# Window attention in a two-stage transformer kernel: the masks are added by VectorE in PSUM instead of by TensorE, with a new order of the work on the engines

## What is computed

```python
qkv = x @ Wqkv
q, k = l2norm(q) * qs, l2norm(k) * ksc
q = q * cos * scale + rotate_half(q) * sin * scale
k = k * cos * inv + rotate_half(k) * sin * inv
...
mask = (it < jb) | (it > jb + w) | (jb == -1)
sim = jnp.einsum('bhwie,bhwje->bhwij', bq, bk2) * QK_SCALE
sim = jnp.where(mask, -jnp.finfo(sim.dtype).max, sim)
attn = jax.nn.softmax(sim, -1)
out = jnp.einsum('bhwij,bhwje->bhwie', attn, bv2)
```

## Time and profile before

| | us |
|---|---|
| median of 3 runs (range) | 3487.71 (3485.86 to 3488.28) |
| time of the profiled execution | 3485.04 |
| its span, first to last instruction | 3483.2 |
| PE matmul busy, of the span | 3410.3 |
| DVE busy | 2991.3 |
| ACT busy | 3056.1 |
| POOL busy | 2494.3 |

### The profile page before, as it was taken

The page is one execution under the profiler, slowest core; times in us unless marked ns, Lnnn a source line. Parts: engine busy times, 40 slices in busy tenths (PEclk is TensorE's granted clock), DMA queues, the critical chain, the costliest instruction groups (busy, mean ns, idle before and its releaser), DMA issues. The chain is left out here.

```text
span 3483.2 us, 177745 instructions
## 1 busy us (share of the span) xinstructions
PE 3410.3 (98%) x70388; PEld 2881.8 (83%) x70388; DVE 2991.3 (86%) x7016; ACT 3056.1 (88%) x10549; POOL 2494.3 (72%) x2057
## 2 busy tenths in 40 slices
PE   8999999999999999999999999999999999999998
PEld 5666677888888888888888888888888888888877
DVE  8999988888888888888888888888888888888886
ACT  8999978898988888888888888888888889888886
POOL 0121178887878878788787887878888788887874
PEclk9999999999999999999999999999999999999999
DMA  2000011111211111121111121111211111111111
GB/s 105 8 5 20 5 53 53 48 42 43 57 55 50 44 44 46 54 57 48 46 44 50 52 57 47 43 42 54 59 48 46 43 47 54 45 46 47 51 42 44
DMA packets 177474, 160.59 MB, mean 46 GB/s; under 512 B 113933, under 2 KB 124813, under 8 KB 176397
## 3 DMA queue, kind: packets, MB, share of 16 engines
q1 hardware_dynamic: 176653, 149.22, 15.2%
HBM read 25.71 MB, written 4.19 MB: 9 GB/s over the span
## 5 line engine op out<-in xcount | busy, mean ns | idle before, releaser
L1544 POOL TENSOR_TENSOR a_rn<-a_ssqc,a_minus_half 128x16 f32<-128x16 f32 x384 | 1113.4, 2900 | 256.3 <-DVE a_ssqc L1751 252.1
L1428 ACT ACTIVATE late<-bank,a_negmax 128x64 f32<-128x64 f32 x3072 | 963.9, 343 | 31.0 <-DVE a_negmax L1705 29.4
L1562 POOL TENSOR_TENSOR a_r<-a_u,a_rn 128x512 f32<-128x512 f32 x768 | 800.7, 1043 | 55.9 <-DVE a_u L1733 10.5
L1428 ACT ACTIVATION_READ_ACCUMULATOR late<-bank,a_negmax 128x1 f32 x3072 | 728.6, 237 | 0.0
L1717 DVE TENSOR_TENSOR a_u<-bank,a_rot_c 128x512 f32<-128x512 f32 x768 | 524.7, 683 | 175.3 <-ACT a_sq L1404 174.7
L1551 POOL TENSOR_TENSOR a_PN<-late,a_erec 128x256 f32<-128x256 f32 x768 | 487.9, 636 | 255.8 <-DVE a_erec L1758 241.4
L1726 DVE TENSOR_TENSOR a_v<-bank,a_rot_s 128x512 f32<-128x512 f32 x768 | 522.7, 681 | 0.0
L1733 DVE TENSOR_TENSOR a_u<-a_u,a_v 128x1024 f32<-128x1024 f32 x384 | 469.7, 1223 | 25.6
L1404 ACT ACTIVATE a_sq<-bank 128x512 f32<-128x512 f32 x768 | 462.8, 647 | 17.2 <-PE bank L1013 16.7
L1411 ACT ACTIVATE a_QK<-bank 128x512 f32<-128x512 f32 x768 | 465.8, 607 | 4.1 <-PE bank L1054 1.9
L1054 PE MATMUL bank<-ident,a_r 128*128 128x128 f32 x3072 | 463.3, 274 | 5.2 <-ACT late L1396 1.8
(11 more groups left out here) (190 smaller groups left out, 7757.2 us busy)
## 6 DMA issues: line engine op xcount, KB each, us to landing
a_V_sh<-a_V_nat SPq DMA_DIRECT2D x384, 192.0 KB, 2.5
a_V_sh<-a_V_nat SPq DMA_DIRECT2D x192, 64.0 KB, 2.4
late<-in_qkv SPq DMA_DIRECT2D x20, 384.0 KB, 3.7
...
```

Of the source, the lines that this page charges most:

```text
L1428: ins = act.activation(E[:, s.par, k, :], scores[:, hp, col:col + KW], ACT.Exp, bias=negmax[:, s.par, k:k + 1], accum_out=esum[:, s.par, k ...
L1544: pool.tensor_tensor(rn[:, a.par, :], ssqc[:, a.par, :], minus_half[:, :], ALU.pow).then_inc(S["rn"], 1)
L1562: pool.tensor_tensor(heads(r[:, a.par, half]), heads(u[:, a.par, half]), rn[:, a.par, mm * 2 * HG:(mm + 1) * 2 * HG].unsqueeze(2).to_broad ...
```

## The change

PE no longer writes the masks; the products of queries and keys now overwrite (`start=True`). DVE has a new instruction per pair, `mask`: it adds a float32 mask (kept in SBUF, loaded as float32, the bf16 copies are gone) to the two banks of scores in place, in PSUM, and `maxima` then waits for it (`masked`). Since one mask now serves 128 rows, the table `windows` holds for the first half of a sequence the first window's form in the first 32 rows. All `cycle` functions but POOL's and SP's have a new order. `sines` of a tile now come ahead of `cosines`, so that `project` also waits for `u_rot`.

```diff
@@ -1007,6 +1002,7 @@
                         pe.wait_ge(S["w_lo"], G * a.layer + a.g + 1)
                     ge(pe, S[f"sq{mm}"], a.k)
                     ge(pe, S[f"v_rot{mm}"], a.k)
+                    ge(pe, S["u_rot"], 2 * a.k - 1 + mm)
                     x, m = n % 2, slice((2 * a.half + mm) * P, (2 * a.half + mm + 1) * P)
                     pe.matmul(p_qk[mm][:, :], xh[:, x, m], wh[:, a.g, 0:2 * CQ], start=True, stop=False)
                     pe.matmul(p_qk[mm][:, :], xl[:, x, m], wh[:, a.g, 0:2 * CQ], start=False, stop=False)
...
@@ -1110,11 +1106,6 @@
                     if s.k == 0:
                         pe.wait_ge(S["pads"], 2)
                     sides = (slice(0, 64), slice(64, P))
-                    for c in range(4):
-                        for e in range(2):
-                            rows = slice(WIN * c, WIN * c + WIN)
-                            pe.matmul(scores[rows, e, :], ident_b[sides[e], 64 * e:64 * e + WIN],
-                                      masks[sides[e], int(s.half > 0 or c > 0), :], start=True, stop=True, skip_group_check=True)
...
@@ -1123,7 +1114,7 @@
                                 for e in range(2):
                                     ins = pe.matmul(scores[WIN * c:WIN * c + WIN, e, col:col + KW],
                                                     QK[sides[e], s.gpar, hp, WIN + first:WIN + first + WIN],
-                                                    QK[sides[e], s.gpar, 2 + hp, first:first + KW], start=False, stop=True,
+                                                    QK[sides[e], s.gpar, 2 + hp, first:first + KW], start=True, stop=True,
                                                     skip_group_check=True)
                     ins.then_inc(S["logits"], 1)
...
@@ -1149,30 +1140,31 @@
                 late_end(n, p)
                 outputs(pair_at(n, p, LAG_O), n * NP + p, done(n, p - 1, LAG_T1))
                 project(n, p, 0)
+                if p == P_VALUES:
+                    up(n, p, 0, 1, p_ta)
+                if p == P_X:
+                    up(n, p, 2, 1, p_ta)
+                if p == P_VALUES:
+                    up(n, p, 1, 1, p_tb)
+                if p == P_GATES:
+                    up(n, p, 1, 0, p_ta)
                 if p == P_GATE:
                     up(n, p, 0, 0, p_ta)
-                if p == P_X:
-                    up(n, p, 2, 1, p_ta)
-                project(n, p, 1)
+                if p == P_X and n + 1 < NI:
+                    transpose_x(n + 1)
+                values(n, p)
                 if p == P_TURN:
                     turn(n)
-                if p == P_VALUES:
-                    up(n, p, 0, 1, p_ta)
-                if p == P_GATES:
-                    up(n, p, 1, 0, p_ta)
-                values(n, p)
                 late_pieces(n, p)
                 if p == P_BIAS:
                     shifts(n)
-                if p == P_X and n + 1 < NI:
-                    transpose_x(n + 1)
-                if p == P_VALUES:
-                    up(n, p, 1, 1, p_tb)
                 if p == P_GATES:
                     up(n, p, 2, 0, p_tb)
                 if p == P_GELU:
                     down(n)
+                project(n, p, 1)
                 if s:
+                    ge(pe, S["exp0"], s.k)
                     ge(pe, S["exp1"], s.k)
                 logits(s, p_s)
...
@@ -1443,32 +1436,32 @@
                     late_outputs(2 * p - 1)
                 queries_and_keys(pair_at(n, p, LAG_Q1), 1)
                 exps(s, 0, 0, p_s)
-                exps(s, 0, 1, p_s)
                 queries_and_keys(pair_at(n, p, LAG_Q0), 0)
                 exps(s, 1, 0, p_s)
                 outputs(pair_at(n, p, LAG_O))
+                exps(s, 0, 1, p_s)
+                squares(n, p, 0)
+                if p == P_X and n + 1 < NI:
+                    high_x(n + 1)
                 exps(s, 1, 1, p_s)
+                if p == P_GATE:
+                    gate_out(n, 0, p_ta)
+                if p < 2:
+                    split_up(n, p)
                 if p == P_TURN:
                     turned(n)
-                squares(n, p, 0)
                 if p == P_GATES:
                     gate_out(n, 1, p_ta)
                 if p == P_GELU:
                     gelu(n)
-                if p == P_GATE:
-                    gate_out(n, 0, p_ta)
-                squares(n, p, 1)
-                if p == P_GATES:
-                    gate_out(n, 2, p_tb)
-                if p == P_X and n + 1 < NI:
-                    high_x(n + 1)
-                values(n, p)
-                probs(pair_at(n, p, LAG_PT))
-                if p < 2:
-                    split_up(n, p)
                 split = split_at(n, p)
                 if split:
                     split_qkv(*split)
+                if p == P_GATES:
+                    gate_out(n, 2, p_tb)
+                values(n, p)
+                squares(n, p, 1)
+                probs(pair_at(n, p, LAG_PT))
...
@@ -1698,9 +1691,16 @@
                     dve.wait_ge(S["w_hi"], G * layer + g + 1)
                     low_weights(dve, A, raw[:, g % 2, :], g).then_inc(S["w_lo"], 1)
 
+            def mask(s, scores):
+                if s:
+                    dve.wait_ge(S["logits"], s.k + 1)
+                    dve.tensor_tensor(scores, scores, masks[:, int(s.half > 0), :].unsqueeze(1).to_broadcast([P, 2, 4 * KW]),
+                                      ALU.add).then_inc(S["masked"], 1)
+
             def maxima(s, scores):
                 if s:
-                    dve.wait_ge(S["logits"], s.k + 1)
+                    dve.wait_ge(S["masked"], s.k + 1)
+                    ge(dve, S["exp0"], s.k - 1)
                     ge(dve, S["exp1"], s.k - 1)
                     dve.tensor_reduce(negmax[:, s.par, :].rearrange("p (b i) -> p b i", b=2), scores.rearrange("p b (i k) -> p b i k", i=4), AX.X,
                                       ALU.max, negate=True).then_inc(S["max"], 1)
...
@@ -1720,7 +1720,10 @@
             def sines(a, mm):
                 if a:
                     m = 2 * a.half + mm
+                    dve.wait_ge(S[f"sq{mm}"], a.k + 1)
                     ge(dve, S["u"], a.k)
...
@@ -1780,40 +1783,41 @@
 
             def cycle(n, p):
                 s, a, b = pair_at(n, p, LAG_S), pair_at(n, p, 0), pair_at(n, p, LAG_R)
-                if p == P_GELU + 1:
-                    feed_forward_out(n)
+                mask(s, p_s)
                 maxima(s, p_s)
                 norms(b)
+                sines(b, 1)
+                clamp(b)
+                if p == P_TURN:
+                    norm(n)
                 cosines(b, 1)
-                clamp(b)
-                sines(b, 1)
+                if p - 1 in (P_TURN, P_GATES, P_GELU):
+                    split_qkv(n, p - 1)
                 if p == P_X:
                     residual(n)
                 if p == P_NORM:
                     stats(n)
+                add(b)
                 if p == P_TURN:
-                    norm(n)
-                add(b)
+                    turned(n)
+                if p == P_VALUES:
+                    product(n, 0, p_ta)
+                reciprocals(s, 0)
+                if p == P_GATES:
+                    split_up(n)
+                if p == P_BIAS:
+                    biases(n)
+                cosines(a, 0)
+                if p == P_X and n + 1 < NI:
+                    low_x(n + 1)
                 if p == P_X:
                     product(n, 2, p_ta)
-                if p == P_VALUES:
-                    product(n, 0, p_ta)
-                if p == P_TURN:
-                    turned(n)
-                cosines(a, 0)
                 sines(a, 0)
-                if p == P_BIAS:
-                    biases(n)
-                if p == P_X and n + 1 < NI:
-                    low_x(n + 1)
+                reciprocals(s, 1)
+                if p == P_GELU:
+                    feed_forward_out(n)
                 if p == P_VALUES:
                     product(n, 1, p_tb)
...
@@ -2006,10 +2012,11 @@
 def tables():
 
     f = np.float32
-    q, k = np.arange(P)[:, None] % 64, np.arange(KW)[None]
+    q, k = np.arange(P)[:, None] % WIN, np.arange(KW)[None]
     seen = (q <= k) & (k <= q + WIN)
 
-    windows = np.stack([np.concatenate([seen & (k >= WIN), seen] * 2, 1), np.concatenate([seen] * 4, 1)], 1)
+    first, later_on = np.concatenate([seen & (k >= WIN), seen] * 2, 1), np.concatenate([seen] * 4, 1)
+    windows = np.stack([np.where(np.arange(P)[:, None] < WIN, first, later_on), later_on], 1)
```

26 lines of the change are left out of this document (10 added, 16 removed).

## The result

| | before | after |
|---|---|---|
| median (runs, range), us | 3486.78 (4, 3485.86 to 3488.28) | 3519.02 (4, 3515.68 to 3520.99) |
| span of the profiled execution | 3483.2 | 3517.6 |

The account below looks back on a forecast made before the run. PE was taken to set the pace, DVE following with little to spare. Eight stretches sum to 62.08 against 61.57 us: +0.51 x 46 = +23, some 4 back, 3504 from 3485.0; median 2.7 above and end-phase masks give 3507 us, range 3447 to 3545.

Parts of the forecast that it names:

- forecast (a): Whole kernel: DVE comes late for the mask at positions 0, 2 and 3; 3507 us, own range 3492 to 3530, chance 0.42.
- The mask add, 0.60 and its own wait 0.19: DVE, every position: the add takes 0.60 us, and maxima wait 0.19 more for its result, starting 0.79 behind it.
- Rival (c): The mask on DVE is dear: 0.80 us and its wait, 0.20 more on five positions, 3553 us; chance 0.09.
- What PE saves, 0.12 x 384 = 46 us: PE ahead of the logits: without mask products it is rid of 0.12 us per pair, 46 us at most.
- Position 1 then takes PE 6.51: PE at position 1: its own work takes 6.51 us once the mask products are gone.
- Position 5, saving nothing for the products ahead of a projection: PE at position 5: projection behind float32 products of `down` takes about 0.1 us longer, so saving counted as nothing; stretch 9.29.
- Rival (d): PE saves nothing, its mask products having filled a switch of number formats: +22 us, 3529 us; chance 0.05.
- The loop, 6.28 + L: Loop over the single `p_s`, logits through ACT's exponentials and copies to the next logits: takes 6.28 us plus DVE's lateness.
- L, how late DVE is: How late DVE comes to the mask: 0.46, 0.15, 1.22 and 1.45 us at positions 0 to 3.
- Position 2, the second projection waiting for the cosines: PE at position 2: second projection waits for DVE's cosines, now behind `norm`, until 7.04 us; stretch 7.83.
- (b): Faster, DVE's lag does not build up: 3467 us, or 3437 if PE alone rules; chance 0.35.
- W: DVE's new work per position, 6.43 us, with extras 7.63 at position 1, 8.06 at 2 and 8.10 at 7.

Follow-up runs that it names:

- run 1: Kernel after with PE's mask products back and DVE's mask gone, so the new order alone: 3487.9 us, ratio 1.000.
- run 3: Kernel after with `mask` left out and nothing masked, for timing only: 3451.6 us, ratio 0.990.
- run 7: As run 1, with ACT's first squares behind the last exponentials except at position 7: 3488.9 us, ratio 1.0013.
- Run 9: New order, masks on PE, values behind PE's second projection at positions 0, 1, 2 and 5, first squares late at 0 to 3: 3539.1 us.
- run 10: Kernel after, DVE's mask kept, with the values behind the second projection at positions 0, 1 and 5: 3512.5 us, ratio 1.0079.
- run 12: run 1 with the values behind the second projection at positions 0, 1 and 5, and squares late at 0 and 1 only: 3458.5 us.
- run 8: run 7 with PE's second projection at position 5 ahead of the float32 products of `down`: 3489.2 us, ratio 1.0014.
- run 4: Kernel after with DVE's norms moved between mask and maxima: 3701.0 us, ratio 1.0615.
- run 5: Kernel after with the mask added to only one of the two score banks, for timing only: 3480.9 us, ratio 0.999.
- run 6: Kernel after with ACT's first squares behind the last exponentials except at position 7: 3539.4 us, ratio 1.0158.

## Why the prediction was right, and where its terms were off

The direction and the mechanism, forecast (a), held: DVE comes late for the mask at positions 0, 2 and 3, PE alone rules at 4 to 7. The time is 12 us above the 3507. That it is so near is in part luck, since errors of both signs cancel. The wait of the maxima was 0.08 shorter than forecast; put into the forecast's own sum this gives 61.7 instead of 62.1, some 18 us less. The loop's closing and the values' wait, both missing or short in the sum, took that back. Point by point:

- **The mask add, 0.60 and its own wait 0.19.** Its duration is 0.689 us. The two together were smaller: mask to maxima is 0.70 to 0.74 by starts, not 0.79 (2013.47 to 2014.17 above). DVE busy 3249 against the 3250 forecast. Rival (c), a dear mask, is out.
- **What PE saves, 0.12 x 384 = 46 us.** Mis-sized: 36 us (run 1 against run 3). Six positions save 0.10 to 0.11, position 0 saves 0.08 and position 3, where DVE is over 1 us late for the maxima in either run, 0.04. That PE's weight loads fill 83% of the span was no sign of free time: 0.10 off a position came off the whole.
- **"Position 1 then takes PE 6.51".** This step failed: without any mask the position takes 6.70. The values, moved up behind the first projection, wait for the copy of the outputs at positions 0, 1, 2 and 5 (in the kernel after at 3 too), which costs 0.14 to 0.16 even where the copy is not late. I had counted that move as free, as the order showed only that the second projection had gone behind them, and had not asked whom the values wait for. At positions 2 and 5 the wait is the whole loss; at 0 and 1 the loop's closing (below) lies 0.02 to 0.05 above it. Shown by runs 7, 9, 10 and 12: with the projection in between, position 5 is 9.29 against 9.45 with PE's masks, and position 1, rid of both, 6.63 against 6.81.
- **Position 5, saving nothing for the products ahead of a projection.** The value, 9.29, was near (9.35), the reason not. A projection behind `down` does take 0.2 longer, but `down` as much less (run 8), so the change of places is free. Run 10 takes the values' wait away and position 5 falls to 9.18, 0.13 under before. Saving and new wait cancelled: the right value by luck. Rival (d), no saving at all, is out by the 36 us.
- **The loop, 6.28 + L.** It holds as a loop (run 4: +3.8 us per iteration; run 5: most of the steady loss gone with half the mask). Its closing constant was short. I forecast 6.74 and 6.56 for positions 0 and 1; they are 6.91 and 6.81. From the first exponential on, ACT's slots are 0.59, 0.57 and 0.49 as reckoned, but from the end of the last slot to the logits it is 0.24 to 0.27, not 0.15. The rest at position 0 is the exponentials' start, 2.87 us into the stretch and not 2.83. At position 1 the loop and the values' wait lie close together: run 10, which takes the latter away, has 6.73. The 0.9 us of room that I gave the loop in the old order was nearer 0.5: at position 1 before, the last sum is read until 5.89 us into the stretch, and PE is ready for its masks at 6.51.
- **L, how late DVE is.** Forecast 0.46, 0.15, 1.22, 1.45 at positions 0 to 3, measured (maxima's distance from the end of the logits, less mask and wake-up) about 0.5, 0, 0.9 and 1.2. Smaller because the maxima follow sooner and because stretches 0 and 1 came out longer and give DVE its time. Hence 2 and 3 at 7.67 and 7.55, not 7.83 and 7.73.
- **Position 2, the second projection waiting for the cosines.** That wait is not far (0.17 us of room: cosines end at 2018.29, the projection starts at 2018.46), but the values' wait for ACT holds PE first. Run 9 shows the cosines' wait by itself, 0.94.
- **Sum.** +0.17, +0.25, -0.16, -0.18, +0.02, +0.06, +0.09, 0.00 against the eight forecast stretches: +0.25, or 10 us over 41 iterations. At the layers' ends 5 us come back (0.74 x 41 = 30 by the medians, 25.3 measured), about the 4 reckoned. The first two and last five iterations lose 6.5 where my sum had 5 x 0.51 = 2.6. Together 10 - 1 + 4 = 13, against the 12 that the time is off by. At position 6 the 0.05 that I gave the earlier copy of the outputs did not come: run 1 has 8.60 there, before 8.57.
- **The rivals.** (b) asked for a lag that does not build up, and named as its condition that W is 0.10 less per position. That was nearly met (0.08), but the loop's closing stood in its place. With half a mask the lag does no harm at 0 and 1: 3480.9. Whoever could halve the add would be at the time of before, and hardly at a gain (ratio 0.999).
- **What would show it.** Right: L1697 near 0.68, DVE near 3250, 2 and 3 longer, 4, 6 and 7 shorter. Wrong: the maxima 0.79 behind; and PE's waits are not put down to exponentials and cosines but to ACT's copy of the outputs (`PE bank L1019`, 23.4 us in 44 waits), the greater part hidden in starts.

**What stays open.** Why a matmul that waits for ACT's copy starts 0.14 behind its end, whether by the wait itself or because its weights are not loaded ahead, was not separated. Why the late squares lengthen position 7 by 0.17 in run 7 and 0.27 in run 6, though not moved there, was not followed beyond DVE's wait. In the first two and last five iterations the order gains 14 us and the mask costs 21, and neither was followed. An order for DVE's mask as free of both waits as run 12 was not tried.
